# The image stage of a token-mixing and expert kernel: shared expert in couples of chunks, and new instruction orders

## What is computed

```python
p = _patchify(x)
pn = (p - mu) * rsqrt(var + EPS) * ln_w + ln_b
out = einsum('bnd,de->bne', pn, W) + b + pos_emd
# scan over l, 16 states per channel
h = dA_i * h + dBu_i
y = einsum('bdn,bn->bd', h, c_i)
# experts
sig = sigmoid(x @ Wg.T); topk_idx = top_k(sig + e_bias, 6)
topk_w = sig[topk_idx] / (sum + 1e-20) * 2.5
routed = sum over chosen experts of topk_w * (silu(x Wg_e) * (x Wu_e)) @ Wd_e
shared = silu(x @ Wsg) * (x @ Wsu) @ Wsd
return x_routed + shared
```

## Time and profile before

| | |
|---|---|
| runs of before, median (lowest to highest) | 4208.4 us (4207.29 to 4208.5) |
| the profiled execution: its own time, its span | 4208.22 us, 4206.5 us |
| busy in the span: PE, DVE, POOL, ACT | 3811 us, 3293 us, 3016 us, 2637 us |
| mean granted clock of PE | 0.967 |
| image stage, expert stage | from about 100 us to about 3180 us, the rest |

### The profile page before, as it was taken

One profiled execution on the slowest core, in us unless ns is written; L12 is line 12 of the kernel. 1 busy time (PEld: TensorE's weight loads), 2 busy tenths in 40 slices (PEclk: granted clock), 3 DMA queues, 4 the chain that ended last, 5 costly groups with the idle time before them and its releaser, 6 DMA issues. The chain is left out here.

```text
span 4206.5 us, 70182 instructions
## 1 busy us (share of the span) xinstructions
PE 3811.3 (91%) x22114; PEld 2887.3 (69%) x22114; DVE 3292.8 (78%) x5523; ACT 2637.3 (63%) x4838; POOL 3015.7 (72%) x1609
## 2 busy tenths in 40 slices
PE   3469999999999999999999999998887999999998
PEld 2346666766666666666676666666556999999997
DVE  1798888888888888888888888888615767777774
ACT  1468888778888778888877888877641222222222
POOL 0888888887888888788888788888503666666665
PEclk8669999999999999999999999999998999999999
DMA  3323333333333333333333332333106888888886
GB/s 84 89 77 91 82 92 96 82 97 96 84 84 96 88 92 87 94 84 92 96 80 95 97 88 79 95 80 81 43 13 157 208 208 208 209 208 208 208 207 140
DMA packets 245505, 472.68 MB, mean 112 GB/s; under 512 B 41692, under 2 KB 164128, under 8 KB 245268
## 3 DMA queue, kind: packets, MB, share of 16 engines
q1 hardware_dynamic: 205840, 429.90, 38.2%
q0 software_dynamic: 36864, 37.98, 5.9%
q10 hardware_dynamic: 2564, 1.82, 0.2%
HBM read 404.99 MB, written 64.56 MB: 112 GB/s over the span
## 5 line engine op out<-in xcount | busy, mean ns | idle before, releaser
L497 POOL TENSOR_TENSOR y<-y,state 128x972 f32<-128x972 f32 x448 | 1006.6, 2247 | 338.6 <-DVE state L658 333.0
L476 POOL TENSOR_TENSOR state<-du,b_rows 128x972 f32<-128x972 f32 x512 | 1195.9, 2349 | 4.7
L652 DVE TENSOR_TENSOR_SCAN ps<-ps,state 128x972 f32<-128x972 f32 x512 | 1113.5, 2180 | 58.6 <-ACT ps L520 43.1
L520 ACT ACTIVATE ps<-delta,a_neg 128x324 f32<-128x324 f32 x1536 | 727.5, 521 | 356.6 <-DVE state L658 299.6
L658 DVE TENSOR_TENSOR state<-ps,c_rows 128x972 f32<-128x972 f32 x512 | 597.8, 1168 | 36.3 <-DVE ps L652 1.8
L1032 POOL DMA_INDIRECT out_rows<-yo,scatter_idx x256 | 369.5, 1443 | 298.4 <-DVE scatter_idx L1115 240.1
L772 PE MATMUL ps<-ws_d,inter 116*98 116x192 f32 (+1 forms) x3072 | 532.8, 327 | 3.5 <-ACT h L542 2.3
L772 PEld LDWEIGHTS ps<-ws_d,inter 116*98 116x98 f32 (+1 forms) x3072 | 495.5, 174 | 12.0 <-issue 8.4
L744 DVE TENSOR_TENSOR inter<-ag,ps 116x648 f32<-116x648 f32 x256 | 211.5, 826 | 314.4 <-PE ps L757 312.6
L754 PE MATMUL ps<-x2f,ws_u 128*116 128x324 f32 x1024 | 345.2, 461 | 48.4 <-ACT ag L628 46.9
L754 PE MATMUL ps<-x2f,ws_g 128*116 128x324 f32 x1024 | 337.1, 452 | 26.9 <-DVE inter L744 22.3
(11 more groups left out here) (174 smaller groups left out, 7362.9 us busy)
## 6 DMA issues: line engine op xcount, KB each, us to landing
b_rows<-bc_rows SPq DMA_DIRECT2D x256, 324.0 KB, 5.0
c_rows<-bc_rows SPq DMA_DIRECT2D x256, 324.0 KB, 5.6
w_lo<-in_we_up SPq DMA_DIRECT2D x128, 348.0 KB
w_down<-in_we_down SPq DMA_DIRECT2D x128, 336.0 KB
x_in<-in_x SPq DMA_DIRECT2D x32, 1176.0 KB, 7.4
w_hi<-in_we_up SPq DMA_DIRECT2D x256, 116.0 KB
image_cnt<-running_counts SPq DMA_DIRECT2D x256, 81.0 KB
w_lo<-in_we_up SPq DMA_DIRECT2D x128, 116.0 KB
```

What stands on the lines that cost most here:

```text
L476: nc.gpsimd.tensor_tensor(b.state[n % 4][:], b.du[t.p][:], row, ALU.mult).then_inc(input_ready, 1)
L497: nc.gpsimd.tensor_tensor(y, y, b.state[n % 4][:], ALU.add).then_inc(y_added, 1)
L520: ins = nc.scalar.activation(to[:, c * L:c * L + L], b.delta[t.p][:, c, :], ACT.Exp, scale=b.a_neg[:, c, k:k + 1])
L652: nc.vector.tensor_tensor_scan(s, s, b.state[k % 4][:].rearrange("p a t -> p (a t)"), 0.0, ALU.mult, ALU.add).then_inc(scan_done, 1)
```

## The change

The shared expert now runs in couples. G k and G k + 1 follow each other, each Silu has its own buffer `ag`, and U k and U k + 1 follow when both Silus are done; one table load serves two Silus. U k of an even chunk waits for the second Silu, U k + 1 for D k.

`to_exp` stays at one place of eight. Three guards go from DVE to ACT (`Identity` with a bias of EPS or 2e-20 / SCALE, tile `small`). `weigh` becomes a sum, a scaling on ACT (piece `den`), and a reciprocal written in place (piece `factor`). The small vectors of the Newton step and of the embedding's statistics go to spare columns of the two PSUM scan buffers (`held` names the one that is held at that time). The tile `zeros` goes; `gt` is used in its place. All five lists of `ORDER` are new. The eight dummies stay.

```diff
@@ ORDER, ACT list, its end
-        ... ("bc_values", -1, 0), ("up_g", 2, 5), ("gate", 1, 0), ("decay", 0, 13), ("gate", 1, 1), ("to_exp", 2, 5), ("step", -1, 0), ("decay", 0, 14),
+        ... ("step", -1, 0), ("decay", 0, 13), ("decay", 0, 14), ("up_g", 2, 6), ("gate", 1, 1),
+        ("up_g", 2, 7), ("to_exp", 2, 7), ("step", -1, 1), ("step", -1, 2)
@@ ACT
+                    elif kind == "den":
+                        act.wait_ge(den_summed, t.v + 1)
+                        nc.scalar.activation(b.top8[:, :, 1], b.top8[:, :, 0], ACT.Identity, bias=b.small[:, 1:2], scale=1.0 / SCALE).then_inc(den_scaled, 1)
                     elif kind in ("ln1_stats", "ln2_stats"):
                         m = int(kind[2]) - 1
+                        act.wait_ge(ln_mean[m], t.v + 1)
+                        nc.scalar.activation(stat[:, m + 1, 4, :], b.mean_var[m][:, :, 1], ACT.Identity, bias=b.small[:, 0:1]).then_inc(ln_var[m], 1)
                         rsqrt_guess(m + 1, 128, 6, ln_var[m], ln_log[m], ln_r0[m], t)
                     elif kind == "up_g":
-                        nc.scalar.preload_act_table_set(SILU_SET)
-                        wait(act, inter_ready, NJ * t.v + k)
+                        if k % 2 == 0:
+                            nc.scalar.preload_act_table_set(SILU_SET)
+                        wait(act, inter_ready, NJ * t.v + k - k % 2)
                         act.wait_ge(g_full, NJ * t.v + k + 1)
-                        nc.scalar.activation(b.ag[:], gu_ps, ACT.Silu).then_inc(ag_ready, 1)
+                        nc.scalar.activation(b.ag[k % 2][:], gu_ps, ACT.Silu).then_inc(ag_ready, 1)
@@ DVE
-            def newton(m, rows, cols, link):
+            def newton(m, rows, cols, piece, link, to):
                 s = stat[0:rows, m, :, 0:cols]
-                link(nc.vector.tensor_tensor(s[:, 0, :], s[:, 5, :], s[:, 5, :], ALU.mult))
-                link(nc.vector.scalar_tensor_tensor(s[:, 1, :], s[:, 0, :], -0.5, s[:, 4, :], ALU.mult, ALU.mult))
-                link(nc.vector.scalar_tensor_tensor(s[:, 3, :], s[:, 1, :], 1.5, s[:, 5, :], ALU.add, ALU.mult))
-                return s[:, 3, :]
+                p = [spare[held(piece)][0:rows, 8 * q:8 * q + cols] for q in range(4)]
+                link(nc.vector.tensor_scalar(p[0], s[:, 5, :], -0.5, None, ALU.mult))
+                link(nc.vector.tensor_tensor(p[1], p[0], s[:, 5, :], ALU.mult))
+                link(nc.vector.tensor_tensor(p[2], p[1], s[:, 4, :], ALU.mult))
+                if to is None:
+                    nc.vector.scalar_tensor_tensor(s[:, 3, :], p[2], 1.5, s[:, 5, :], ALU.add, ALU.mult)
+                    to = p[3]
+                link(nc.vector.scalar_tensor_tensor(to, p[2], 1.5, s[:, 5, :], ALU.add, ALU.mult))
+                return to
...
-                        link(ins)
-                        nc.vector.tensor_scalar(stat[:, m + 1, 4, :], b.mean_var[m][:, :, 1], EPS, None, ALU.add).then_inc(ln_var[m], 1)
+                        ins.then_inc(ln_mean[m], 1)
...
-                            link(nc.vector.tensor_reduce(den, b.ch[:], AX.X, ALU.add))
-                            link(nc.vector.tensor_scalar(den, den, 2e-20, None, ALU.add))
-                            link(nc.vector.reciprocal(b.top8[:, :, 1], den))
-                            nc.vector.tensor_scalar(b.x2[:, :, :, D], b.top8[:, :, 1].rearrange("p (b k) -> p b k", b=2), SCALE, None, ALU.mult).then_inc(factor_ready, 1)
+                            nc.vector.tensor_reduce(den, b.ch[:], AX.X, ALU.add).then_inc(den_summed, 1)
+                    elif kind == "factor":
+                        dve.wait_ge(den_scaled, t.v + 1)
+                        nc.vector.reciprocal(b.x2[:, :, :, D], b.top8[:, :, 1].rearrange("p (b k) -> p b k", b=2)).then_inc(factor_ready, 1)
@@ PE
                     elif kind == "up_g":
-                        wait(pe, inter_ready, NJ * t.v + k)
+                        if k % 2 == 0:
+                            wait(pe, inter_ready, NJ * t.v + k)
+                        else:
+                            pe.wait_ge(ag_ready, NJ * t.v + k)
                         up(b.ws_g, t, k).then_inc(g_full, 1)
                     elif kind == "up_u":
-                        pe.wait_ge(ag_ready, NJ * t.v + k + 1)
+                        if k % 2 == 0:
+                            pe.wait_ge(ag_ready, NJ * t.v + k + 2)
+                        else:
+                            pe.wait_ge(inter_ready, NJ * t.v + k)
```

More of the change, by code:

```diff
@@ L68 @@
-        ("x1_turn", -1, 2), ("up_u", 2, 4), ("bc_values", -1, 0), ("up_g", 2, 5), ("gate", 1, 0), ("warm", 2, 4), ("gate", 1, 1), ("step", -1, 0),
-        ("up_u", 2, 5), ("step", -1, 1), ("up_g", 2, 6), ("warm", 2, 5), ("step", -1, 2), ("up_u", 2, 6), ("warm", 2, 6), ("up_g", 2, 7), ("warm", 2, 7),
-        ("up_u", 2, 7), ("warm", 1, 0)
+        ("warm", 3, 4), ("down_a", 3, 0), ("down", 3, 0), ("up_g", 2, 0), ("count", 2, 0), ("down_a", 3, 1), ("down", 3, 1), ("resid", 1, 0),
+        ("down_a", 3, 2), ("resid", 1, 1), ("down", 3, 2), ("up_g", 2, 1), ("resid", 1, 2), ("emb_a", -2, 0), ("up_u", 2, 0), ("count", 2, 1),
@@ L71 @@
+        ("step", -1, 1), ("up_u", 2, 6), ("step", -1, 2), ("up_u", 2, 7)
     ),
     "act": (
-        ("decay", 0, 0), ("decay", 0, 1), ("down", 3, 0), ("decay", 0, 2), ("emb_a", -2, 0), ("resid", 1, 0), ("down", 3, 1), ("decay", 0, 3),
-        ("emb_stats", -1, 0), ("decay", 0, 4), ("resid", 1, 1), ("down", 3, 2), ("up_g", 2, 0), ("decay", 0, 5), ("resid", 1, 2), ("decay", 0, 6),
-        ("to_exp", 2, 0), ("count", 2, 0), ("ln2_stats", 1, 0), ("up_g", 2, 1), ("count", 2, 1), ("to_exp", 2, 1), ("emb_a", -2, 1), ("emb", -2, 0),
@@ L76 @@
[L76 to L79, removed]
@@ L80 @@
-        ("decay", 0, 15), ("step", -1, 1), ("up_g", 2, 6), ("to_exp", 2, 6), ("step", -1, 2), ("softplus", -1, 0), ("up_g", 2, 7), ("to_exp", 2, 7)
+        ("softplus", 0, 0), ("decay", 1, 15), ("down", 3, 0), ("decay", 0, 0), ("emb_a", -2, 0), ("decay", 0, 1), ("count", 2, 0), ("den", 2, 0),
+        ("down", 3, 1), ("decay", 0, 2), ("resid", 1, 0), ("up_g", 2, 0), ("emb_stats", -1, 0), ("decay", 0, 3), ("down", 3, 2), ("resid", 1, 1),
+        ("decay", 0, 4), ("decay", 0, 5), ("resid", 1, 2), ("up_g", 2, 1), ("ln2_stats", 1, 0), ("count", 2, 1), ("emb_a", -2, 1),
@@ new lines @@
+        ("ln2_apply", 1, 0), ("decay", 0, 6), ("x2_turn", 1, 0), ("emb", -2, 0), ("decay", 0, 7), ("ln1_stats", -1, 0), ("up_g", 2, 2),
+        ("x2_turn", 1, 1), ("up_g", 2, 3), ("decay", 0, 8), ("ln1_apply", -1, 0), ("decay", 0, 9), ("x2_turn", 1, 2), ("decay", 0, 10),
+        ("x1_turn", -1, 0), ("up_g", 2, 4), ("x1_turn", -1, 1), ("up_g", 2, 5), ("x1_turn", -1, 2), ("decay", 0, 11), ("bc_values", -1, 0),
+        ("decay", 0, 12), ("emb", -2, 1), ("gate", 1, 0), ("step", -1, 0), ("decay", 0, 13), ("decay", 0, 14), ("up_g", 2, 6), ("gate", 1, 1),
@@ L86 @@
[L86 to L89, removed]
+        ("up_u", 3, 6), ("fill_c", 1, 14), ("choose", 2, 0), ("up_u", 3, 7), ("choose", 2, 1), ("scan", 1, 15), ("choose", 2, 2), ("weigh", 2, 0),
@@ L131, in use_number, with held @@
     return use
+def held(piece):
+    open_scans = []
+    for kind, _, k in ORDER["dve"]:
+        if (kind, k) == piece:
+            return open_scans[-1] % 2
+        if kind == "scan":
+            open_scans.append(k)
+        elif kind == "fill_c" and k in open_scans:
+            open_scans.remove(k)
 def run_bodies(engine, body):
@@ L201, in __init__ @@
         self.y = two("y", [128, 3, L])
-        self.ag = sb("ag", [HC, 2, L])
+        self.ag = two("ag", [HC, 2, L])
         self.inter = sb("inter", [HC, NJ, 2, L])
@@ L206, in __init__ @@
         self.mask = sb("mask", [128, 6, E], BF16)
+        self.small = sb("small", [128, 2])
         self.top8 = sb("top8", [128, 6, 8])
@@ L297, in _ @@
                 nc.vector.memset(b.upto[:], 1.0).then_inc(filled, 1)
+                step(nc.vector.memset(b.small[:, 0:1], EPS))
+                step(nc.vector.memset(b.small[:, 1:2], 2e-20 / SCALE))
                 step(nc.vector.memset(b.ones[:], 1.0))
@@ L353, in phase1 @@
     state_ps = [flat[:, 1024 * r:1024 * r + 3 * L] for r in range(2)]
+    spare = [flat[:, 1024 * r + 3 * L:1024 * r + 1024] for r in range(2)]
     gu_ps = ps[0:HC, 4:6, 0:L]
@@ L363, in phase1 @@
     ln_var = [sem(f"ln{k}_var") for k in (1, 2)]
+    ln_mean = [sem(f"ln{k}_mean") for k in (1, 2)]
+    den_summed, den_scaled = sem("den_summed"), sem("den_scaled")
     ln_log = [sem(f"ln{k}_log") for k in (1, 2)]
@@ L381, in phase1 @@
     waited = sem("waited")
-    LINKS = {"emb": 6, "ln1": 5, "ln2": 5, "choose": 4, "weigh": 4}
+    LINKS = {"emb": 7, "ln1": 5, "ln2": 5, "choose": 4, "weigh": 1}
     chains = {k: sem(f"chain_{k}") for k in LINKS}
@@ L516, in body @@
                             act.wait_ge(du_ready, t.v + 1)
+                        if k < 2 and isinstance(t.v, int) and t.v == 0:
+                            act.wait_ge(emb_var, 2)
```

68 lines of the change are left out of this document (36 added, 32 removed).

## The result

The changed kernel takes 4239.7 us (median of 4 runs, 4235.48 to 4242.67) against 4208.4: 0.7% slower, ratio 1.0074 with an interval of 1.0057 to 1.0092. The forecast was 4188, so the direction was wrong, and the time lies at the upper end of the range. The profiled execution took 4235.5 us with a span of 4233.8, 27.3 more than before.

The account below looks back on a forecast made before the run. No engine is full, so a loop of handoffs bounds the period; 90.5 us a pair, 0.7 less than 91.18, times 29 periods gives 20 us, with ramp and drain 0: 4188 us, range 4138 to 4244.

Parts of the forecast that it names:

- The walk: Step-by-step sum of one image-stage period in the new order, Silu 6 to Silu 6: 90.5 us, 0.7 less than 91.18.
- stretch C: From the end of ln1's inverse root, through Silu 2, G3, U2 and D2, to G4: ends at 68.6 us.
- G3 2.1: The gate products G3 on PE, right behind Silu 2, priced at 2.1 us.
- the term for ramp and drain: Time outside the 29 full periods: taken as 0, between -4 and +4 us.
- Table loads: ACT's loads fall from 18 to 14 a period at 1.28 us, but each inverse root gets two, 2.5 us longer.
- 3.9 us a pair: How much lower the period's sum would be if Ln then Exp cost one load in the three inverse roots.
- The drain: Extra ACT time per table load; with it four fewer loads would be worth 10.7 us; the prediction counted none.
- Rival 1: In A, choose's first step waits for POOL's addition, delaying D7 and the loop 1.8 us: 4240 us, 28%.
- PSUM for the small vectors: Cost of small DVE steps now writing to PSUM: 0 to 3 us a pair on the path, taken as 0.
- DVE's work: DVE's busy time per period falls by 4.3 us, to about 76; by itself worth nothing.
- Predicted waits: DVE waits before scan 3 (2 to 3 us), at D2 for U2 (3.5) and at D4 (2.3).
- Rival 2: Inverse roots off the path, so the period falls to PE's content, 88.5 us: 4130 us, 12%.

Follow-up runs that it names:

- run 1: Changed kernel with one of its eight dummies moved from behind G3 to the gap ahead of it: 4205.9 us, ratio 0.9996 to the kernel before.
- run 2: Changed kernel with two more dummies, ten a pair, both in the gap ahead of G3: 4207.5 us, ratio 1.0001 to the kernel before.
- Run 3: Changed kernel with explicit loads of the set holding Ln and Exp put back behind Silu 0 and Silu 1: 4080.5 us, ratio 0.970.
- run 7: Kernel before without its explicit loads of the set holding Ln and Exp behind Silus 0 to 6: 4426.6 us, ratio 1.0527.
- run 8: Run 3 with the two guards of the layer norms moved back from ACT to DVE: 4126.2 us, ratio 0.9801 to the kernel before.
- run 9: Changed kernel with one explicit load of the set holding Ln and Exp, behind Silu 1: 4108.9 us, ratio 0.9763 to the kernel before.

## Why the prediction was wrong, point by point

**The walk held, but for one term.** Stretches of the kernel after, from the end of Silu 6 at 1554.58 to the next one's at 1646.62:

| stretch | ends at | us, forecast | us, measured |
|---|---|---|---|
| A, to scan 3 | 1586.70 | 31.7 | 32.1 |
| B, to ln1's inverse root | 1610.30 | 23.5 | 23.6 |
| C, to G4 | 1625.37 | 13.4 | 15.1 |
| D, PE alone | 1639.45 | 14.3 | 14.1 |
| E, to Silu 6 | 1646.62 | 7.3 | 7.2 |
| handoffs rounded away | | 0.3 | in the above |
| period | | 90.5 | 92.0 |

**The step that failed** is in stretch C: "G3 2.1". It took 3.65 us, at a granted clock of 0.53. The same stretch had told me that PE would stand idle in front of G3, since in the walk G3 begins only when Silu 2 has ended, and I priced what comes behind that idle time with a row taken from a trace in which PE never waits over 0.8 us. The last part of the prediction names a granted clock under 1.00 as what would break all of it, and still it had no rival and no chance. With 1.65 us more in C the sum is 92.15, 0.97 over before, and 29 x 0.97 = 28 us: slower, 4236. Runs 1 and 2 show that this is what made the change a loss: without it the time is that of before. They show too how small the gain was: with G3 at full clock in most periods 90.43 us a period, but 4206 us, no different from before. The commonest period of the kernel before is 91.15, so like for like the gain is the 0.7 us of the walk. But 27 periods of 90.43 instead of the mean of 91.26 are 22 us; of these, longer single periods take 9 (the mean from D7 to D7 is 90.78), what follows the full periods 9, and little is left. So even with the failed term put right the time would have been that of before within 8 us, not 20 us under it: the term for ramp and drain, taken at 0, was a loss of 8 in run 1.

**Table loads.** 14 a period of 1.28 us, two in each inverse root: right. The choice to trust the program's order over the one load of the Trainium skill (ScalarE: Activation LUTs, "Table sets: the hidden batching unit") was right for this kernel. What I did not ask was what that difference would be worth if it were taken away: I noted "3.9 us a pair" and went on. Run 3 measured it: 5.6 us a pair with the clock's part, 159 us, five times what the change lost.

**The drain** of about 1.38 us that the Trainium skill (ScalarE: Activation LUTs, "What ACT_TABLE_LOAD costs") puts on top of each load: run 7's rows show none, Ln begins 1.30 us after the start of its load, and the load 0.02 us after the end of the decays. The measurement decides.

**Rival 1** (the choice meets POOL's addition) had 28% and came within 0.3 us of the measured time, for another reason. The collision did not come: the first step is L741, 0.95 us, in the group rows of ten periods, and D7 starts 1.2 us after it.

```profile
L741 DVE SCALAR_TENSOR_TENSOR ch<-gt,e_bias 128x768 f32<-128x768 f32 x10 | 9.5, 948 | 0.0
...
L671 DVE TENSOR_TENSOR ps<-ps,stat 128x6 f32<-128x6 f32 x20 | 3.4, 172 | 0.7
...
L670 DVE TENSOR_SCALAR ps<-stat 128x6 f32<-128x6 f32 x20 | 3.1, 154 | 13.3 <-ACT stat L528 13.3
```

A time inside a rival's price is no evidence for the rival.

**PSUM for the small vectors**: taken at 0 between 0 and 3 us; the rows above are 0.15 to 0.17 us, so 0 was right, and these steps do not wait for POOL, as the guard of run 8 does: of the 96 L670s of the kernel after 37 ran while POOL was busy, none over 0.17 us. **DVE's work**: 73.2 us, not 76; the choice's first step (2.97 to 0.95) and the mask (L718 before, 1.37; L752 after, 0.60) also lost their wait for POOL, and my sum had neither. **Predicted waits**: scan 3 2.5 us (2 to 3 forecast), D4 2.35 (2.3), D2 5.8, not 3.5; of the difference 1.6 us go with the clock, since D2 waits 4.15 us in runs 1 and 2, and the other 0.7 are the walk's own error. **Ramp and drain** at 0 between -4 and +4: 3.0 gained in the ramp and 6.1 lost behind the full periods, 3.1 lost in all. "Two chunks 11.7 instead of 11.9" was wrong, they take 11.94.

**Rival 2** (the period falls to PE's content, 88.5 us) was refused rightly for this change and is what run 9 (87.5 us) and run 3 (86.25) reach; its estimate of 2 to 3 us that PE cannot avoid was too high, run 3 has under 2.

## What to carry to other kernels

When a walk of the new order finds a wait of TensorE that is longer than any in the trace of before, price what stands behind it at both clock levels, and give the slow one a chance: here a wait of 2.3 us cost another 1.65 in one kernel and mostly nothing in another. Look for dummy work that stands one block behind such a wait, where it protects nothing. Where two functions share a table set but the compiler chooses the loads, load the common set by hand in front of the first; and when a change removes such loads, test that element by itself before anything else.
